# Four zero products of TensorE moved from ahead of q's first sum to behind its first three sums

## The reference

```
q_emb = relu(cond @ W3 + b3)                       # 64 x 1024
v_sum = sum(x, axis=1)                             # 64 x 1 x 1024
y = (128 * x + v_sum) * q_emb[:, None, :]          # 64 x 128 x 1024
out = x + relu(y @ W2 + b2)
```

## Time and profile before

| | |
|---|---|
| median of 3 runs | 635.45 us (635.14 to 635.71) |
| span of the profiled execution | 633.3 us |
| PE busy in it | 627.9 us (99%) |
| DVE, ACT, POOL busy | 445.8, 418.3, 12.3 us |

### The profile page before, as it was taken

One profiled execution on the slowest core, in us unless ns is written; L12 is line 12 of the kernel. 1 busy time (PEld: TensorE's weight loads), 2 busy tenths in 40 slices (PEclk: granted clock), 3 DMA queues, 4 the chain that ended last, 5 costly groups with the idle time before them and its releaser, 6 DMA issues.

```text
span 633.3 us, 9252 instructions
## 1 busy us (share of the span) xinstructions
PE 627.9 (99%) x2791; PEld 518.3 (82%) x2791; DVE 445.8 (70%) x683; ACT 418.3 (66%) x897; POOL 12.3 (2%) x16
## 2 busy tenths in 40 slices
PE   9999999999999999999999999999999999999997
PEld 7788888888888888888888888888888888888886
DVE  4899979676766757687576776757677576776533
ACT  3888896839576594856839577594856839577320
POOL 3130000000000000000000000000000000000000
PEclk9999999999999999999999999999999999999999
DMA  8925746554353734337354353744336353350703
GB/s 325 401 114 199 249 150 219 182 195 161 134 174 132 253 145 142 125 164 232 132 198 144 133 187 132 239 158 132 137 161 232 132 199 135 140 189 1 243 22 132
DMA packets 26654, 108.83 MB, mean 172 GB/s; under 512 B 2960, under 2 KB 3600, under 8 KB 22800
## 3 DMA queue, kind: packets, MB, share of 16 engines
q1 hardware_dynamic: 26208, 108.41, 48.1%
q10 hardware_dynamic: 432, 0.27, 0.2%
HBM read 75.11 MB, written 33.55 MB: 172 GB/s over the span
## 4 chain that ended last, share of the span: by engine, by line
PE 98%; DVE 1%; POOL 1%; ACT 0%; issue 0%; DVEq 0%
PE acc L293 98%; PE acc L310 1%; POOL x_sb L584 1%; DVE a_lo L673 0%; DVE xn L868 0%; ACT a_hi L391 0%; DVE x_sb L634 0%; DVE w_lo L689 0%; ACT q_emb L475 0%; DVE scale L610 0%; DVE warm L733 0%; DVEq L57 0%; DVE bias L612 0%
## 5 line engine op out<-in xcount | busy, mean ns | idle before, releaser
L293 PE MATMUL acc<-w_hi,a_hi 128*128 128x512 f32 x904 | 352.1, 389 | 0.9 <-DVE a_lo L673 0.9
L293 PE MATMUL acc<-w_hi,a_lo 128*128 128x512 f32 x904 | 351.7, 389 | 0.0
L293 PE MATMUL acc<-w_lo,a_hi 128*128 128x512 f32 x904 | 351.7, 389 | 0.0
L409 ACT ACTIVATE x_sb<-x_sb,bias,scale 128x128 f32<-128x128 f32 x492 | 203.2, 487 | 11.6 <-DVE bias L612 11.6
L293 PEld LDWEIGHTS acc<-w_hi,a_hi 128*128 128x128 f32 x904 | 169.7, 188 | 36.8 <-DVE a_lo L673 1.5
L293 PEld LDWEIGHTS acc<-w_hi,a_lo 128*128 128x128 f32 x904 | 169.7, 188 | 35.2
L293 PEld LDWEIGHTS acc<-w_lo,a_hi 128*128 128x128 f32 x904 | 169.7, 188 | 35.1
L684 DVE TENSOR_TENSOR a_lo<-x_sb,a_hi 128x512 fp32r<-128x512 f32 x150 | 103.5, 690 | 106.3 <-ACT a_hi L404 105.6
L404 ACT CAST a_hi<-x_sb 128x512 fp32r<-128x512 f32 x150 | 93.3, 622 | 38.7 <-PE acc L293 37.3
L404 ACT CAST a_hi<-s 128x512 fp32r<-128x512 f32 x60 | 37.4, 623 | 74.3 <-PE acc L293 69.1
L606 DVE TENSOR_REDUCE vsum<-x_sb 128x16 f32<-128x2048 f32 (+1 forms) x38 | 73.6, 1942 | 6.5 <-DMA x_sb<-x_t 6.5
(11 more groups left out here) (48 smaller groups left out, 188.2 us busy)
## 6 DMA issues: line engine op xcount, KB each, us to landing
xn<-x SPq DMA_DIRECT2D x64, 512.0 KB, 4.1
out<-xn SPq DMA_DIRECT2D x62, 512.0 KB, 3.3
x_sb<-x_t SPq DMA_DIRECT2D x30, 1024.0 KB, 4.9
x_sb<-w_t SPq DMA_DIRECT2D x4, 512.0 KB, 6.3
x_sb<-x_t SPq DMA_DIRECT2D x4, 512.0 KB, 10.7
u_sb<-w_q SPq DMA_DIRECT2D x3, 512.0 KB, 5.9
m_sb<-w_q SPq DMA_DIRECT2D x3, 512.0 KB, 6.0
out<-xn SPq DMA_DIRECT2D x3, 256.0 KB, 2.9
```

Source lines behind the costliest of these rows:

```text
L293: return nc.tensor.matmul(dst, lhs, rhs, start=False, stop=False, skip_group_check=True)
L409: last = nc.scalar.activation(x_sb[:, slot, h, t, k], x_sb[:, slot, h, t, k], ACT.Identity, bias=bias[:, slot, h, t, k:k + 1], scale=scale ...
```

## The change

The loop of four zero products ahead of the first q sum goes. The number of zero products behind the sums 0, 1 and 2 becomes 3, 2 and 2 in place of 1, 1 and 1. There are seven after the eight of L310 both before and now, and `marked` is still raised by the last of them.

```diff
             for n in range(8):
                 nc.tensor.matmul(acc[:, n], warm[:, :P], warm[:], start=True, stop=True)
-            for _ in range(4):
-                keep_warm()
             pe.wait_ge(small_loaded, 16)
             for k in range(KT - 2):
                 q_sum(k)
-                if k < 3:
+                for _ in range((3, 2, 2, 0, 0, 0)[k]):
                     last = keep_warm()
             last.then_inc(marked, 1)
```

## The result

| | before | changed |
|---|---|---|
| median | 635.33 us (22 runs) | 635.37 us (22 runs) |
| lowest, highest | 634.53, 635.74 | 634.98, 643.97 |
| ratio, 95% interval | | 1.0026 (1.0014 to 1.0037) |

The two medians agree within 0.04 us, and yet the ratio, which goes by the mean, lies clear of 1. The 22 times of the changed kernel say why. Fourteen lie between 634.98 and 635.39; I call them short. Seven lie between 638.84 and 639.22, and one at 643.97; those are the long ones. Before has none above 635.74. So the change does next to nothing to a typical execution. In seven of 22 it costs 3.8 us (median of the seven against median of the short ones), and in one 8.7 us.

What follows compares the result with a forecast made beforehand. PE, busy 627.9 of 633.3 us, was taken as the bound, so a later end of sum 3 delays the end. Sum 3's +0.23 to +0.35 us, taken as +0.25 on 635.45, gave 635.7 us, range 635.1 to 637.2.

Steps and rivals of the forecast that it cites:

- The size of the shift: End of q sum 3 on PE: predicted +0.23 to +0.35 us later, of which 0.15 to 0.35 us reaches the end.
- What POOL would give back: POOL's four tiles before PE's long row: could give back at most 0.37 of the shift, so 0.63 to 1 passes on.
- Rival 3: Shift at sum 3 swallowed between 10 and 17.5 us as POOL's tiles get faster: 635.45 us, chance 0.05.
- Rival 2: Start of q sums: data lands earlier and sums don't mind the low clock; gain of 0.40, 635.05 us, chance 0.07.
- Rival 1: Gap ahead of q's sums makes PE's clock rise later: +0.87 to +4.2 us, 636.7 us taken, chance 0.22.
- sums that hardly mind: Late-clock estimate: q sums hardly slow at the lower level, with five zero products slow: 636.7 us.
- the rise is 3 us later: PE's clock at the start: the late-clock case decides from a rise 3 us later than before.
- the evidence against it: Against a late clock: PE kept the higher level through sums and a 0.9 us gap; three runs agreed within 0.57 us.

Runs made afterwards that it cites:

- the first long execution: First of two further profiled executions of the unedited changed kernel that were long: 639.04 us.
- the long hole: Changed kernel with one more wait, for W3's second piece, ahead of q's first sum: ratio 1.0096 (1.0055 to 1.0137), six of eight executions long.
- fewer zero products: Kernel before with two zero products ahead of the sums in place of four, one still behind each of sums 0 to 2: median 634.79 us, ratio 0.9993.
- two ahead and none behind: Kernel before with two zero products ahead of the sums in place of four and none behind them: ratio 0.9999, nine at 634.10 to 634.92 us, three at 636.39 to 636.90.
- ten then a gap: Changed kernel with two zero products back ahead of the sums, 2, 2, 1 behind, plus a wait for W3's second piece: ratio 1.0072, five of 12 long.
- four ahead and none behind: Kernel before with its four zero products ahead of the sums kept and none behind them: median 634.81 us, ratio 0.9993.
- two of the four ahead: Changed kernel with two zero products back ahead of q's first sum and 2, 2, 1 behind sums 0 to 2: 634.65 to 635.82 us, ratio 1.0001.
- the four gone: Kernel before without the four zero products ahead of the sums, nothing added behind: ratio 1.0041, five of 12 long at 641.26 to 641.78 us.

## Why the prediction was right, and where it wasn't

**The median, and no change: right.** 635.37 us lies within 635.1 to 637.2, 0.33 under the 635.7 forecast; the difference to before, 0.04, is no change. The step that carried it held: PE's order ahead of sum 3 only trades a covered wait for an open one, and the shift goes through every link one for one.

**The size of the shift: right in the trace, by terms that were off in pairs.** +0.23 to +0.35 was worked out, +0.30 measured. But the gap was 0.3 us, not 0.65, as the load landed at 4.85; in other profiled executions it landed between 4.8 and 5.3. And sum 0 cost 0.49 more than at the higher level, not 0 to 0.12: it started 0.40 us earlier at the lower level, its records doubled, and the clock rose at 5.70, not 5.53. The two errors cancel, and that is luck. In the medians of many runs next to nothing is left of the 0.30. Before's own executions spread over 1.5 us, and the rise of the profiled ones lies anywhere from 4.05 to 5.78, so one profile of each kernel can't carry tenths.

**What POOL would give back: nothing.** The share passed on was put at 0.63 to 1; it was 1. Rival 3, which lived on it, falls by the trace. Its time, 635.45, is nearer to the measured median than the 635.7 of the forecast, so the time alone would not have told them apart.

**Rival 2: half of it came.** The load did land earlier, by 0.39 of the 0.65 us. But sums do mind the lower clock, and the doubled records of sum 0 ate what the landing gave.

**Rival 1: the mechanism right, its size and its chance wrong.** A late clock was named with 0.22 and 1.29 us. It came in 14 of 36 executions and cost 3.7 to 3.8 us as a rule. Three steps of it failed. First, "sums that hardly mind": a q sum nearly doubles at the lower level, 1.60 us against 0.83 (sum 0, with its start, 1.76), and three of them cost 2.5 us more than in the profile before. The estimate had this end, +4.2 with all seven products and three doubled sums, and in the first long execution PE's long row does start 3.99 later than before (21.55 against 17.56). I chose against it from the weight loads of the bf16 products, the wrong rows: those of the sums are float32, and their starts stretch too, to 0.21 apart at the lower level against 0.11. Second, "the rise is 3 us later": in the two profiled long executions it was 5.1 and 7.6 us later, with sums mixed with zero products in between. Third, the evidence against it. That PE kept the higher level through the sums says nothing about rising through them; the long hole shows a lower level that lasts through all eight. And the agreement of the runs before was read as one moment of rise that they share. There is none: ahead of any difference between the kernels the clock had risen at 4.05 in one profile and not before 5.52 in another. Before has wide products up to 5.92, past every rise seen in a short execution, so there a rise that comes earlier or later moves the end by less than a microsecond (estimate: half of the 1.5 us between those two).

**What it needs, by the runs.** Gap and sums together: gap and dense products behind it, 0 long of 11; sums behind eight zero products and no gap, 0 of 11; sums behind ten, with a gap only if the rise comes early, 0 of 22; gap and sums, 14 of 36 and 5 of 12; a longer gap, 6 of 8, and 5 of 12 even behind ten. With ten ahead and none behind the sums there is another way to lose: the clock falls again in 3 of 12, at 2 us. The Trainium skill ("TensorE: Matmul & The Clock Gate", Part 1 on the HAM clock gate) has sustained activity release the throttle, and says that the moment of release varies between executions of a kernel; by that rule the traces agree, with rises at 4.05 to 5.78 us in the eleven short profiled executions of this case, and at 10.63, 13.1 and 26.94 in the three long ones. What sets apart a short from a long execution of the same kernel isn't shown by any run here. One reading fits the rows and is argued only: the rise of a short execution can be due until 5.8; the change ends the wide products at 4.59, and an execution in which it is due after that depends on what the gap and the first sum leave. In the two short profiles of the changed kernel the gap was also the smaller, 0.31 and 0.34 us by the starts against 0.55 and 0.64 in the long ones, and four executions can't tell the two apart.

**Form of the forecast.** A single time and range for the median took the rival as an alternative for all executions. It was a share of the executions. The forecast should have said that rival 1 can come in some executions and leave the median alone; the mean moved by 0.26% where the median moved by nothing.

## To carry to other kernels

Zero products that bridge the start are worth most where TensorE would otherwise idle before its clock is up, so place them across the wait for the first data; two over this gap did the job of four as long as others stood between the sums (0 long of 22), and four right behind the wait worked as well (0 of 11). Look at the list of times, not just at the median: a change at the start can be neutral in three executions of five and cost several microseconds in the others. Before pricing a late clock, find what the small float32 matmuls cost at the lower level, since they nearly double, like the wide ones. And read the moment of the rise from more than one profile.

## What the hardware showed that I had not expected

- The granted clock reads full in the views ahead of the rise, even where the steps say 1.2 GHz, because the trace's record starts with the rise. A mean clock of 1.0 therefore doesn't exclude a late rise (639.04 us, clock 1.000), while a mean of 0.995 says that the clock fell after one. The first row is of the longer hole, 12 to 18 us, with PE busy throughout at 0.21 us a sum record; the second is of the first long execution of the changed kernel, 5 to 13 us. Columns: stretch and length, then busy time and count of PE, PEld, DVE, ACT, POOL, then the clock, the DMA share and GB/s.

```profile
12.00:18.00 6.00, 6.00 (x29) 5.63 (x28) 1.72 (x7) 2.02 (x5) 1.41 (x2) 1.00 1.03 406
```

```profile
5.00:13.00 8.00, 7.86 (x31) 6.58 (x32) 1.28 (x2) 1.14 (x3) 0.00 (x0) 1.00 1.02 399
```

- Behind the same start at 1.20 us and the same row of wide products, the record has the rise at 4.05, 4.23, 4.56, 4.93, 5.15 and 5.52 us in six executions in which PE had no gap up to then (in this order: fewer zero products, two ahead and none behind, ten then a gap, four ahead and none behind, two of the four ahead, before).
- The length of a small gap doesn't decide alone. By the starts it was 0.55 and 0.64 us in the two long executions of the changed kernel and 0.71 in the short one with the four gone, in which the clock rose at 5.23, inside the gap.
- The records of a q sum (float32, 128x64) start 0.11 us apart at the higher level and 0.21 at the lower; the first step of a sum is about half of that, so eight of them take 0.84 and 1.60 us.
